# Inner rows of the spectrum contiguous in DRAM, 128-channel pieces of three kinds for the inner transform and mixing, the second normalisation on ScalarE, and a new order of the work

## The reference

```python
# block 1: depthwise 7x7 convolution, normalisation over channels, MLP 96 -> 384 -> 96, residual
h = conv7x7_depthwise(x) + conv_b
h = (h - mean(h)) * rsqrt(var(h) + 1e-5) * ln_g + ln_b
t = (gelu(h @ w1 + b1) @ w2 + b2) * layer_scale + x
# block 2: on tokens; spectral mixing with 192 channels
h = relu(bn1(normalise(t) @ aw1.T))
X = fft(h, axis=tokens, norm="ortho")
xr = relu(X.real * rd - X.imag * id + rb)      # rd, id: diagonals of r and i
xi = relu(X.imag * rd + X.real * id + ib)
t = t + bn2(real(ifft(xr + 1j * xi)) @ aw2.T)
# block 3: MLP with operands rounded to an 8-bit float (5 exponent, 2 mantissa bits)
t = t + qlinear(relu(qlinear(normalise(t), W1, b1)), W2, b2)
```

## Time and profile before

| | |
|---|---|
| median of three runs | 4494.48 us (4490.79 to 4496.14) |
| profiled execution | 4496.04 us, span 4494.2 us |
| busy in the span | TensorE 89%, VectorE 74%, ScalarE 50%, GpSimd 41% |
| granted TensorE clock | 0.948 of full |
| DMA | 532.47 MB, 118 GB/s in the mean |

### The profile page before, as it was taken

One profiled execution on the slowest core, in us unless ns is written; L12 is line 12 of the kernel. 1 busy time (PEld: TensorE's weight loads), 2 busy tenths in 40 slices (PEclk: granted clock), 3 DMA queues, 4 the chain that ended last, 5 costly groups with the idle time before them and its releaser, 6 DMA issues.

```text
span 4494.2 us, 88363 instructions
## 1 busy us (share of the span) xinstructions
PE 4006.1 (89%) x22802; PEld 2904.3 (65%) x22802; DVE 3307.4 (74%) x10713; ACT 2254.2 (50%) x4610; POOL 1840.4 (41%) x2468
## 2 busy tenths in 40 slices
PE   5999958899999999999999999999999999999986
PEld 3444435676666766676667676666666667676764
DVE  2333335688888888888888888888888888888877
ACT  2433423455555555555555555555555555555543
POOL 1111163444444444444444444444444444444431
PEclk9999979999999999999999999999999999999986
DMA  6566633444444444434444444444444444444331
GB/s 174 161 164 176 168 93 89 109 118 118 117 119 117 120 118 116 111 103 111 111 115 112 109 111 111 116 118 120 118 115 119 115 120 120 117 115 115 109 98 53
DMA packets 420415, 532.47 MB, mean 118 GB/s; under 512 B 220047, under 2 KB 378493, under 8 KB 404413
## 3 DMA queue, kind: packets, MB, share of 16 engines
q1 hardware_dynamic: 405920, 510.40, 42.4%
q10 hardware_dynamic: 14272, 20.04, 1.8%
HBM read 295.18 MB, written 235.12 MB: 118 GB/s over the span
## 4 chain that ended last, share of the span: by engine, by line
PE 29%; DVE 26%; DMA 13%; issue 10%; ACT 3%; SPq 2%; POOL 1%; DVEq 1%; ACTq 0%; POOLq 0%
DMA inner<-outer_spectrum 6%; PE psum L989 6%; DMA outer_spectrum<-outer 6%; DVE stats L823 5%; PE psum L1009 5%; PE psum L1028 4%; PE psum L995 4%; DVE minus L898 4%; DVE plus L898 3%; DVE t L859 3%; PE psum L1037 2%; DVE h L932 2%; DVE xn L925 2%; PE psum L1017 2%; DVE act L881 2%
## 5 line engine op out<-in xcount | busy, mean ns | idle before, releaser
L684 POOL TENSOR_TENSOR scales<-sums,minus_half 112x4 f32<-112x4 f32 (+1 forms) x480 | 605.8, 1266 | 1686.2 <-DVE sums L839 1685.7
L726 POOL TENSOR_TENSOR both<-plus,minus 96x224 f32<-96x224 f32 (+1 forms) x1024 | 642.7, 653 | 356.6 <-DVE minus L898 297.8
L781 ACT ACTIVATE uw<-psum,spec 96x224 f32<-96x224 f32 (+1 forms) x1024 | 449.4, 512 | 397.9 <-PE psum L1028 395.9
L989 PE MATMUL psum<-hn,w_sb 96*128 96x448 f32 x1344 | 566.3, 559 | 31.8 <-ACT hn L747 31.8
L995 PE MATMUL psum<-hid,w_sb 128*96 128x448 f32 x1344 | 554.7, 549 | 2.1 <-ACT hid L762 2.0
L762 ACT ACTIVATE hid<-psum,b_sb 128x448 f32<-128x448 f32 x672 | 421.3, 634 | 233.3 <-PE psum L989 192.0
L387 PE MATMUL c_psum<-c_xt,c_toeplitz 128*112 128x448 f32 x1152 | 477.9, 552 | 49.2 <-ACT c_xt L329 26.0
L1028 PE MATMUL psum<-inner_dft,inner 112*96 112x112 f32 x3712 | 431.2, 271 | 90.5 <-DMA inner<-outer_spectrum 89.8
L415 DVE TENSOR_SCALAR c_h<-c_psum,c_bias 112x448 f32<-112x448 f32 x192 | 199.0, 1037 | 415.1 <-PE c_psum L387 415.1
L701 POOL TENSOR_SCALAR h_norm<-h,sums,scales 112x96 f32<-112x96 f32 x896 | 461.3, 531 | 103.2 <-PE psum L982 102.9
L1028 PEld LDWEIGHTS psum<-inner_dft,inner 112*96 112x96 f32 x3712 | 406.0, 173 | 110.9 <-issue 86.4
(11 more groups left out here) (85 smaller groups left out, 6615.0 us busy)
## 6 DMA issues: line engine op xcount, KB each, us to landing
outer_spectrum<-outer SPq DMA_DIRECT2D x448, 168.0 KB
inner<-outer_spectrum SPq DMA_DIRECT2D x32, 2016.0 KB
c_xpad<-x SPq DMA_DIRECT2D x96, 392.0 KB, 11.2
h_tokens<-c_h SPq DMA_DIRECT2D x24, 1568.0 KB, 8.4
h<-h_tokens SPq DMA_DIRECT2D x32, 1176.0 KB, 13.9
x_sb<-x SPq DMA_DIRECT2D x32, 1176.0 KB, 7.7
residual_stream<-t SPq DMA_DIRECT2D x224, 168.0 KB, 2.0
inner_inverse<-unmixed SPq DMA_DIRECT2D x224, 168.0 KB, 2.3
```

What stands on the lines that cost most here:

```text
L684: nc.gpsimd.tensor_tensor(scales[which][:, at:at + w], su[:, :, 5], minus_half[:, 0:w], ALU.pow).then_inc(ready.sem, 1)
L726: last = nc.gpsimd.tensor_tensor(both[:, c % 2, m, 0:w, k * PT // 2:(k + 1) * PT // 2], half(plus), half(minus), ALU.subtract if k else AL ...
L781: last = nc.scalar.activation(uw[:, j % 2, k, 0:w * PT // 2].rearrange("p (s k) -> p s k", s=w), re, ACT.Identity, bias=spec[:, m, shift:s ...
L989: pe.matmul(bank("M1", c, m, CW, 128), w1_sb[:, m * 128:(m + 1) * 128], hn[:, c * CW:(c + 1) * CW], start=True, stop=True).then_inc(m1_mad ...
```

## The change

- `outer_spectrum` becomes (28, 116, 192), position outermost. The rows of the outer transform are ordered so that four groups of 29 (each two frequency parities x two parts, the last padded with a zero column) are contiguous for a position: 116 rows instead of 114. A chunk is stored by two DMAs whose runs are one 192-value row each, and `inner` is read by two DMAs with one run per partition: 8 pairs first, then the other 21.
- The inner transform takes 128 channels at a time. Two pairs are 384 columns, so three kinds of pieces: channels 0 to 127 of the first, channels 128 to 191 of the first with 0 to 63 of the second, and channels 64 to 191 of the second. 12 jobs of up to four pieces for 16 of up to four. `spec` and `aw2` hold their values once for each kind. The mixing has, for two pairs, two products of 96 columns and one of 192 whose stationary operand is the middle piece.
- The second normalisation is scale times row plus offset by ScalarE; GpSimd makes the offset, scale times minus the mean, after the power.
- The outer transform's matrix is loaded into spare room of the convolution's result tile and copied into the new order by VectorE, before the convolution's sums.
- All numbers of `STAGES` and `LATER` are new.

In the diff what repeats on the other engines is left out (plus, minus, `both` and the reads of PSUM go by the new job numbers), as are sizes and the loads of `spec` and `aw2`.

```diff
@@ -23,6 +23,10 @@
 K1 = PT // 2 + 1
 NS = (K1 + 1) // 2
 ND = (NS + CH - 1) // CH
+NG = (ND + 1) // 2
+PAIRS = 4
+KINDS = 3
+ROWS = 4 * NS
 CC = 4
 NPART = C // CC
...
+def blocks(g, kind):
+    pairs = min(PAIRS, NS // 2 - PAIRS * g)
+    return pairs + (NS % 2 if g == NG - 1 and kind < 2 else 0)
 class Signal:
...
 STAGES = {
-    1: {"M1": (-0.5, 11.7, NC), "M2": (6.0, 11.8, NC), "T": (12.5, 11.7, NC), "W1": (22.0, 11.9, NC),
-        "A": (25.5, 12.7, NC)},
-    2: {"B": (8.0, 8.7, ND), "W": (18.0, 9.9, ND), "IB": (27.5, 8.9, ND)},
-    3: {"AP": (2.0, 11.1, NC), "S2": (6.5, 11.0, NC), "N2": (12.5, 11.4, NC), "T2": (17.5, 10.8, NC),
-        "F1": (21.0, 12.0, NC), "G": (23.5, 11.8, NC), "F2": (31.0, 12.1, NC)},
-    "next": {"L0S": (35.5, 3.9, NC), "L0N": (94.5, 4.0, NC), "HT": (88.5, 3.0, NC)},
-    "fetch": {"FETCH": (28.5, 10.5, NC - 3)},
-    "fetch next": {"FETCH NEXT": (103.0, 1.4, 3)},
+    1: {"M1": (0.0, 11.9, NC), "M2": (5.0, 11.5, NC), "T": (14.0, 11.8, NC), "W1": (23.0, 11.5, NC),
+        "A": (32.5, 11.9, NC)},
+    2: {"B": (0.5, 4.3, KINDS * NG), "W": (16.5, 9.7, ND), "IB": (28.0, 8.9, ND)},
+    3: {"AP": (-5.0, 11.5, NC), "S2": (8.0, 10.6, NC), "N2": (17.0, 11.0, NC), "T2": (17.5, 11.0, NC),
+        "F1": (18.5, 11.7, NC), "G": (20.5, 10.3, NC), "F2": (33.5, 11.4, NC)},
+    "next": {"L0S": (35.5, 6.2, NC), "L0N": (127.5, 2.9, NC), "HT": (102.0, 2.1, NC)},
+    "fetch": {"FETCH": (-18.5, 10.5, NC - 3)},
+    "fetch next": {"FETCH NEXT": (95.0, 3.8, 3)},
 }
 LATER = {
-    "act": {"F2": 0.5, "T2": -1.0, "B": -0.5, "IB": -0.5, "HT": 0.5, "A": 0.5},
-    "dve": {"B": 1.0, "M2": 0.5, "T": 2.5, "F2": 9.0, "S2": 1.5, "L0N": 0.5, "G": -0.5, "N2": -0.5, "L0S": -10.0},
-    "pool": {"B": 6.5, "T": 5.0, "S2": 5.0, "L0N": -21.0, "L0S": -7.5},
-    "sp": {"M2": -2.0, "IB": -0.5, "A": 12.0, "FETCH": -8.0, "FETCH NEXT": 10.5},
+    "act": {"F2": 1.5, "T2": 0.5, "B": 1.5, "IB": 1.0, "HT": 7.0, "A": 1.0, "S2": 1.5, "W": 1.0, "F1": 1.0, "M1": 1.0, "N2": -2.0},
+    "dve": {"B": 1.5, "M2": 1.0, "T": -0.5, "F2": 3.5, "S2": 3.0, "L0N": -17.5, "G": 8.0, "N2": -11.0, "L0S": -6.0, "AP": 0.5},
+    "pool": {"B": 4.5, "T": 0.5, "S2": 6.5, "L0N": -49.0, "L0S": -4.0},
+    "sp": {"M2": 20.5, "IB": 12.0, "A": 15.0, "FETCH": -12.0, "FETCH NEXT": 3.0},
     "pe": {},
 }
...
+    g_dram = nc.dram_tensor("outer_spectrum", (NQ, ROWS, H2), F32, kind="Internal").ap()
     v_dram = nc.dram_tensor("inner_inverse", (NS, PT, C), F32, kind="Internal").ap()
     f_dram = nc.dram_tensor("row_filters", (BR, C, WINDOW * TAPS), F32, kind="Internal").ap()
...
             sp.dma_start(bias[:, :], bass.AP(conv_b.tensor, 0, [[0, PT], [1, C]])).then_inc(consts_loaded, 16)
-            sp.wait_ge(pads_zeroed, 2)
+            sp.wait_ge(pads_zeroed, 3)
             load_x(0, 0)
+            sp.dma_start(transform, fa_c.rearrange("p q m -> p (q m)")).then_inc(transform_loaded, 16)
             load_x(1, 1)
...
+            dve.wait_ge(transform_loaded, 16)
+            columns = transform.rearrange("p (q m) -> p q m", m=2 * K1)
+            for j in range(2):
+                for part_ in range(2):
+                    at, count = NS * (2 * j + part_), NS - j
+                    nc.vector.tensor_copy(wts.outer_dft[0:PT, :, at:at + count],
+                                          columns[:, :, K1 * part_ + j:K1 * (part_ + 1):2])
+                    if j:
+                        nc.vector.memset(wts.outer_dft[0:PT, :, at + count:at + NS], 0.0)
             def part(n, g, slot, has_next, has_second):
...
-        outer = sb("outer", [2 * K1, 2, CH, H2])
-        uw = sb("uw", [C, 2, 2, CH * PT // 2])
-        plus = sb("plus", [C, 2, 2, CH * PT // 2])
-        minus = sb("minus", [C, 2, 2, CH * PT // 2])
-        both = sb("both", [C, 2, 2, CH, PT])
+        outer = sb("outer", [ROWS, 2, CH, H2])
+        uw = sb("uw", [128, 2, 2, PAIRS * PT // 2])
+        plus = sb("plus", [128, 2, 2, PAIRS * PT // 2])
+        minus = sb("minus", [128, 2, 2, PAIRS * PT // 2])
+        both = sb("both", [128, 2, KINDS, PAIRS, PT])
         mixed = sb("mixed", [PT, 2, CH * C])
         unmixed = sb("unmixed", [PT, 2, CH, C])
...
                         sp.wait_ge(outer_done.sem, outer_done.at(n, 2 * c + 1))
-                        for rows, part in ((slice(0, PT, 2), slice(0, K1 - 1)), (slice(1, PT, 2), slice(K1, 2 * K1 - 1)),
-                                           (slice(PT, 2 * K1), slice(K1 - 1, 2 * K1, K1))):
-                            sp.dma_start(g_dram[rows, CH * c:CH * c + CH, :], outer[part, c % 2, :, :]
+                        for rows in (slice(0, PT), slice(PT, ROWS)):
+                            sp.dma_start(g_dram[CH * c:CH * c + CH, rows, :].rearrange("q m h -> m q h"), outer[rows, c % 2, :, :]
                                          ).then_inc(outer_stored[c % 2].sem, 16)
                     if name == "A" and c == NC - 1:
@@ -642,11 +666,10 @@
                             sp.wait_ge(s.sem, s.at(n))
                             sp.sem_inc(passed, 1)
                         sp.wait_ge(spec_made.sem, spec_made.at(n))
-                        for part, (first, end) in enumerate(((0, CH), (CH, NS - 1))):
-                            rows = bass.AP(g_dram.tensor, first * PT * H2, [[H2, PT], [PT * H2, end - first], [1, H2]])
-                            sp.dma_start(inner[:, first:end, :], rows).then_inc(inner_loaded[part].sem, 16)
-                        sp.dma_start(inner[0:2 * NQ, NS - 1, :], g_dram[2 * K1 - 2:2 * K1, :, :].rearrange("m q h -> (m q) h")
-                                     ).then_inc(inner_loaded[1].sem, 16)
+                        spectrum = g_dram.rearrange("q (r s) h -> (q r) (s h)", s=NS)
+                        first = 2 * PAIRS * H2
+                        for part, columns in enumerate((slice(0, first), slice(first, NS * H2))):
+                            sp.dma_start(inner[:, columns], spectrum[:, columns]).then_inc(inner_loaded[part].sem, 16)
                     if name == "IB":
                         if c == 0:
...
@@ -712,21 +735,25 @@
                         pool.wait_ge(xn2_done.sem, xn2_done.at(*before(n, c, NC, 2)))
                         deviation(2, c, ln2_ready)
+                        pool.wait_ge(ln2_ready.sem, ln2_ready.at(n, c))
+                        pool.sem_inc(passed, 1)
+                        at = slice(CH * (c % 2), CH * (c % 2) + CH)
+                        nc.gpsimd.tensor_tensor(offsets[:, at], scales[2][:, at], sums[2][:, :, 3], ALU.mult
+                                                ).then_inc(ln2_offset.sem, 1)
                     if name == "B":
-                        w = chunk_pairs(c)
-                        pool.wait_ge(mix_made.sem, mix_made.at(*before(n, c, ND, 2)))
-                        for m in range(2):
-                            j = 2 * c + m
...
                                        bank("S2", c, 0, CH * C, PT)).then_inc(rows2_done.sem, 1)
+                    if name == "N2":
+                        act.wait_ge(ln2_offset.sem, ln2_offset.at(n, c))
+                        act.wait_ge(xt2_made.sem, xt2_made.at(*before(n, c, NC, 2)))
+                        for j in range(CH):
+                            at = CH * (c % 2) + j
+                            last = nc.scalar.activation(xn2[:, c % 2, j, :], t2_rows[:, c % 2, j, :], ACT.Identity,
+                                                        bias=offsets[:, at:at + 1], scale=scales[2][:, at:at + 1])
+                        last.then_inc(xn2_done.sem, 1)
                     if name == "T2":
                         act.wait_ge(xt2_made.sem, xt2_made.at(n, c))
...
                             pe.wait_ge(act1_done.sem, act1_done.at(n, 2 * c + m))
-                            dst = bank("A", c, m, 2 * H2, 2 * K1)
+                            dst = bank("A", c, m, 2 * H2, ROWS)
                             for j in range(2):
                                 last = pe.matmul(dst[:, j * H2:(j + 1) * H2], outer_dft[:, CH * c + 2 * m + j, :],
                                                  act1[:, (2 * c + m) % 4, j, :], start=True, stop=True)
                             last.then_inc(outer_made.sem, 1)
                     if name == "B":
-                        if c < 2:
-                            pe.wait_ge(inner_loaded[c].sem, inner_loaded[c].at(n - 1))
-                        w = chunk_pairs(c)
-                        for m in range(2):
-                            dst = bank("B", c, m, w * PT, C, "spec")
-                            for s in range(w):
-                                last = pe.matmul(dst[:, s * PT:(s + 1) * PT], inner[:, CH * c + s, m * C:(m + 1) * C],
-                                                 inner_dft[:, :], start=True, stop=True)
-                            last.then_inc(spec_made.sem, 1)
+                        g, kind = c // KINDS, c % KINDS
+                        if c % KINDS == 0 and g < 2:
```

(28 more changed lines are left out.)

159 lines of the change are left out of this document (80 added, 79 removed).

## The result

The changed kernel takes 4539.8 us, the median of four runs (4533.3 to 4545.8), and the kernel before, on the same chip, 4495.3 (4490.8 to 4496.5). The ratio is 1.0097 with a 95% interval of 1.0082 to 1.0113: it is slower, where 4300 us was forecast. The profiled execution has a span of 4544.0 us, 49.8 more than before, at a mean granted clock of 0.921 for 0.948.

The account below looks back on a forecast made before the run. TensorE was taken to set the pace, with waits at the seam. Per turn matmuls -2.3, idle -3.0, clock -1.0 made 110.4 us for 116.7; 30 turns -189, ends -6: 4300 us, range 4180 to 4440 (forecast alone 4240 to 4370).

Parts of the forecast that it names:

- Bounds and the middle of the turn: Mid-turn TensorE sets the pace and VectorE is full too; 9.5 us a turn of TensorE idle, nearly all at the seam.
- Rival C: Slower: ScalarE's in-order wait at N2 holds copies that empty TensorE's banks; about 4550 to 4720 us; chance 0.10.
- rival B: New head of the turn: `back` lands 10.5 us after issue for 7.6, delaying AP0, M1, B0; 4425 us; chance 0.20.
- Part 1: Fewer, wider matmuls in inner transform and mixing: 2.3 us a turn less, ends at 2.1 and 3.6.
- Part 2: Elementwise work: VectorE falls from 97 to 80 us a turn, ScalarE at most 77, GpSimd at most 56; costed at nothing mid-turn.
- Part 3: DRAM layout: the big inner read holds SyncE's queue under 1 us for 5.12; its second piece is needed over 20 us later.
- Rival D: The layout does nothing: small store pieces cost what long reads save, last store 7 us for 3.75; 4400 us; chance 0.05.
- Part 4: Order at the seam: AP0 waits 4.8 us, B0 1.6; seam idle about 6.0, with 0.5 in the middle, against 9.5.
- The ScalarE wait for a DMA goes: At the seam, ScalarE's wait on the outer-spectrum store vanishes, with the x load ahead of A4's store.
- 5.2 us after IB7 is done: At the seam, the time at which the load of `back` is issued; AP0 then comes at 12.8 us.
- The inner read at 13 us: At the seam, the last outer store waits behind `back` until 13 us; a 4.5 us read lets B0 start at 17.5.
- 3 us for 4: Clock loss per turn: one 5 us stop with a short one behind it costs less than three stops; 1.0 us less.

Follow-up runs that it names:

- experiment ten: Changed kernel with the step times of the kernel before, except new times for the inner-transform jobs and the mixing: 4628.9 us, 1.0316 of the kernel before.
- experiment one: Changed kernel with the x load moved from ahead of an outer store to between the two inner reads: 4405.9 us, 0.9795 of the kernel before.
- experiment three: Changed kernel with AP0 moved behind the first M1, on TensorE only: 4539.5 us, 1.0091 of the kernel before.
- both moves: Changed kernel, x load between the two inner reads, chunk 5's outer store ahead of the wait for the last inner-inverse store and `back` load: 4375.9 us, 0.9752.
- Experiment nine: Changed kernel with the second normalisation back on VectorE, at the new table's time: 5309.1 us; in a second kernel 2.5 time units earlier: 4522.9 us.

## Why the prediction was wrong, and where it was right

**Bounds and the middle of the turn: right.** TensorE is full there (19.84 of 20.00 us from 2320 on) and VectorE has room. Rival C, the slower case by ScalarE's N2 in the middle, did not happen: the waits for xn come to 16.1 us from 1000 to 4000 us, 0.6 a turn (5.5 us in the same stretch before). The result is slower by another mechanism, which no rival had in full; rival B comes nearest.

**Part 1, the matmuls: right in size.** Eight inner records take 2279.60 - 2278.69 = 0.91 us, 114 ns each; two others of the same view give 110 and 112. I took 112. With the same 112 moving columns a record took 96 ns at 96 weight columns. The rule of the Trainium skill, "TensorE: Matmul & The Clock Gate", section "LDWEIGHTS (loading the stationary operand)", gives a weight load of 128 columns 107 ns, a little less than a record took. By its rule the time grows with the weight columns, and the trace agrees in that. Two pairs' mixing takes 2286.06 - 2285.34 = 0.72 us by the six records, exactly the 98 + 98 + 164 ns twice.

**Part 2: right, and worth what I said, nothing.** VectorE went from 97 to 2396.99 / 3374 x 117.57 = 83.5 us a turn (80 forecast), ScalarE to 69.7 (at most 77), GpSimd to 51.4 (at most 56).

**Part 3: right that the long read is cheap to issue.** Both inner reads take 0.79 us of SyncE's time for 5.12 and 0.87. The wait for the inner rows moved from the second transform to the first and hardly shrank (74.5 us in all for 89.8), since the read itself is issued late. Rival D, dearer stores with 768-byte pieces, is not what happened: the last store does take as long as D feared (7 us and more), but by the table of experiment ten its time goes with the distance of the load of `back` ahead of it, and with that load 6.7 us or more ahead both kinds of pieces take 3.1 to 3.4 us.

**Part 4: here the prediction fails, in four steps.** (1) "The ScalarE wait for a DMA goes, since the x load now stands ahead of A4's store, two chunks before the ring is full." The opposite: the wait is 119.3 us for 98.0, and the x load is its cause (experiment one). I counted the slots of `outer` and didn't count what the store queues behind. The trace of before had it too, the x load issued 0.44 us ahead of a store (timeline of SyncE, not among the rows that the prediction read), with the 95.0 us of waits at the end of it:

```profile
2224.32 0.33 SPq L595 DMA_DIRECT2D x_sb<-x  x1
2224.76 1.56 SPq L637 DMA_DIRECT2D outer_spectrum<-outer  x3
```

(2) "5.2 us after IB7 is done" for the issue of `back`: it was 10.1 us (2256.36 after 2246.3). I took the time from the old seam; in the new order IB7's store is issued behind the x load and an outer store, and SyncE waits 6.9 us from its issue, for 4.7. Its landing from the issue was near the 7.6 I took: AP0 starts 8.2 us after it. So rival B was right that the queue's line moves everything, and wrong in its price (10.5 us) and its cause: AP0 first costs nothing (experiment three). (3) The inner read at 13 us: 20.4. A6's copy ends 9.9 us after IB7 for 7.5, the outer stores are behind the late `back` and take 9.0 us to the read's issue (2266.74 - 2257.70), where the forecast left the last one 5.5, and the read goes 2.2 us after `back` has let AP0 start (2266.74 for 2264.58). (4) The clock: "3 us for 4". Three stops one after another left TensorE at the low level (0.50 granted) from 2256 to 2268, and again near 2272 to 2275 behind the last of them, and the mean at 0.93. The whole is 0.07 x 117.6 = 8.2 us a turn, part of it in idle time. Filling two of the waits gave back 1 us of it; with both moves, and so shorter waits, the mean is 0.96 again.

**The sum.** Forecast 110.4 us a turn, measured 117.6: 7.2 off. Idle is 10.8 us a turn (310.5 / 3374 x 117.6) for 6.5, 4.3 of it; the rest, 2.9, lies in busy time. I put it down to the clock, since the groups that ran at full clock took what was forecast; no run separates it. Part of the idle time was a slip of addition: my waits of 4.8 and 1.6 us make 6.4, and I carried 6.0. The read called 688 KB is 672 KB in the profile's units, twice 336, and landed after 5.1 us (B0's start) for 4.5. The low end of the forecast's own range comes to about 4225 by its terms, not 4240; none of the three matters beside 240 us. With both moves the period is 112.0 and idle 7.3, so the queue's order accounts for 5.5 of the 7.2 by experiment. What stays is the wait for the inner rows behind `back`; another order of the two ends was not tried.

The trailing turns cost 15.4 us more where I allowed 5: their chain through single chunks now goes through ScalarE's N2, and TensorE waits there for xn 43.2 us, for 14.9 before. Experiment nine bears this out in part: in its second kernel, with N2 on VectorE, the same stretch takes 4500.9 - 4333.73 = 167.2 us for 176.6, and the wait is 33.8 us. In experiment ten, with N2 on ScalarE and nearly the old step times, it takes 163.5. So engine and order both enter, and ScalarE's N2 alone isn't the cause of the 15.4. The 5.3 us at the start are about the 5 that I named for the four copies if they came late, but the copies aren't their cause: they and the two memsets are done by 21.6 us, and the convolution's first sums start at 57.26 us, for 57.48 before. The convolution ends 6.4 us later (626.0 for 619.6 us), and why isn't known.

## What to carry to other kernels

When a step waits for a store, add up the bytes that stand ahead of it in the same queue, not only the slots of its ring; a load that nobody needs soon belongs behind the transfers that release an engine. In an in-order queue a wait in the middle delays every issue behind it, so time a seam by the queue's list, wait by wait, before timing it by the compute engines' lists. Taking work from an engine that wasn't late bought nothing here, and an order tuned for one kernel has to be looked at anew when the jobs in it change.

## What the runs showed of the hardware

A store of 348 KB issued 0.44 us behind a load of 1176 KB released its buffer after 9.2 us, and an inner-inverse store of 42 KB let the queue go on after 6.9 us with that load ahead and after 2.3 without. From the issue of the last outer store to that of the read which waits for it, it took 3.1 to 3.4 us where a load of 1176 KB had been issued 6.7 us or more before the store, in runs of 3072 bytes or 768, and 6.9 to 9.4 us where it had been issued about 2 us before. A group of f32 matmuls behind a stop took 3.67 us at a granted clock of 0.50, for 2.43 at full clock. And an order that is 2.5 time units off in one engine's table turned 4523 us into 5309, with a mean clock of 0.878 for 0.925.
